# The recurrence's two projections as three products of rounded halves, in place of one 32-bit product

## The reference, cut to what matters

```
y      = layernorm(x1)                                # (8, 512, 256)
v      = y @ W_write.T                                # "values", 256 -> 256
read_t = alpha * sum over s < t of gamma^(t-1-s) * (y_t . y_(s-1)) * v_s       # in each head
s      = y + read @ W_read.T                          # "mix", 256 -> 256
```

## Time and profile before

| | us |
|---|---|
| median of 3 runs (3278.1 to 3281.41) | 3280.44 |
| the profiled execution | 3278.38 |
| its span, first to last instruction | 3276.6 |
| recurrence phase, from its first instruction to the first of the next phase | 1977.8 to 2152.8 |
| TensorE busy over the span | 3081.6 (94%) |

### The profile page before, as it was taken

One profiled execution on the slowest core, in us unless ns is written; L12 is line 12 of the kernel. 1 busy time (PEld: TensorE's weight loads), 2 busy tenths in 40 slices (PEclk: granted clock), 3 DMA queues, 4 the chain that ended last, 5 costly groups with the idle time before them and its releaser, 6 DMA issues. The chain is left out here.

```text
span 3276.6 us, 74792 instructions
## 1 busy us (share of the span) xinstructions
PE 3081.6 (94%) x22540; PEld 2326.4 (71%) x22540; DVE 2156.3 (66%) x6507; ACT 1932.9 (59%) x4816; POOL 1154.6 (35%) x1806
## 2 busy tenths in 40 slices
PE   8979999999999999989999997969999965999995
PEld 6756666666666666668888884536666655999995
DVE  4338888888888888876666655547777636333334
ACT  4437777777777777765565553226766653333333
POOL 2104444444444444443333330034242202333331
PEclk9989999999999999999999998979999967999998
DMA  8863332222333233243333342111111133223225
GB/s 265 279 198 83 82 80 82 81 78 79 89 84 81 80 82 81 77 161 117 128 128 135 109 140 66 39 51 31 37 47 36 44 119 103 37 38 89 37 40 172
DMA packets 200831, 309.98 MB, mean 95 GB/s; under 512 B 36242, under 2 KB 144530, under 8 KB 200434
## 3 DMA queue, kind: packets, MB, share of 16 engines
q1 hardware_dynamic: 187826, 290.54, 29.0%
q0 software_dynamic: 12864, 17.57, 3.2%
HBM read 208.03 MB, written 90.31 MB: 91 GB/s over the span
## 5 line engine op out<-in xcount | busy, mean ns | idle before, releaser
L993 POOL TENSOR_SCALAR at_p<-at_p,at_recip 128x512 f32<-128x512 f32 (+3 forms) x1030 | 538.4, 541 | 630.0 <-DVE at_recip L1105 630.0
L1031 ACT ACTIVATE at_p<-at_p,at_nmax 128x512 f32<-128x512 f32 (+3 forms) x1032 | 570.5, 555 | 253.2 <-DVE at_nmax L1099 253.2
L1099 DVE CUSTOM_DVE_ANT_0 at_p<-at_s_ps,at_bias 128x512 f32<-128x512 f32 (+3 forms) x1032 | 459.7, 488 | 56.3 <-PE at_s_ps L1211 39.7
L1211 PE MATMUL at_s_ps<-at_k_twice,at_q 64*128 64x512 f32 (+3 forms) x3096 | 343.6, 341 | 8.2 <-DVE at_nmax L1099 6.7
L2057 DVE CUSTOM_DVE_ANT_0 aa_a_ps<-aa_a_ps,aa_hidden 128x128 f32<-128x128 f32 (+3 forms) x512 | 242.4, 511 | 102.2 <-PE aa_a_ps L2219 100.0
L1233 PE MATMUL at_o_ps<-at_pT,at_v 128*64 128x512 f32 (+3 forms) x2064 | 307.2, 440 | 0.0
L1111 DVE COPY at_pT<-at_t_ps 128x512 f32<-128x512 f32 (+3 forms) x512 | 239.5, 488 | 88.6 <-PE at_t_ps L1223 86.0
L1957 ACT ACTIVATE aa_pT<-aa_b_ps 128x512 f32<-128x512 f32 (+1 forms) x384 | 196.2, 530 | 140.6 <-PE aa_b_ps L2237 138.0
L1223 PEld LDWEIGHTS at_t_ps<-ident,at_p 64*128 64x128 f32 x5120 | 189.0, 138 | 118.0 <-issue 118.0
L1233 PEld LDWEIGHTS at_o_ps<-at_pT,at_v 128*64 128x64 f32 x2064 | 136.9, 137 | 186.5 <-issue 167.9
L663 ACT ACTIVATE nw_h<-nw_h_ps,nw_b 128x512 f32<-128x512 f32 x192 | 132.2, 689 | 211.4 <-PE nw_h_ps L767 211.0
(11 more groups left out here) (325 smaller groups left out, 7443.5 us busy)
## 6 DMA issues: line engine op xcount, KB each, us to landing
at_k_twice<-k_dram SPq DMA_DIRECT2D x260, 256.0 KB, 3.8
k_dram<-ln_keys SPq DMA_DIRECT2D x128, 256.0 KB, 3.8
nw_w_raw<-in_w_all_dram SPq DMA_DIRECT2D x26, 1024.0 KB, 5.0
nw_w_raw<-in_w_all_dram SPq DMA_DIRECT2D x52, 512.0 KB, 6.7
at_v<-v_dram SPq DMA_DIRECT2D x129, 128.0 KB, 2.0
v_dram<-ln_values SPq DMA_DIRECT2D x16, 1024.0 KB, 5.7
w_all<-in_w_dram SPq DMA_DIRECT2D x12, 768.0 KB, 9.2
nw_xh<-xh_dram SPq DMA_DIRECT2D x10, 512.0 KB, 4.4
```

The source lines that it names most:

```text
L993: pool.tensor_scalar(p, p, recip[:, u:u + 1], 1.0, ALU.mult, ALU.mult).then_inc(scaled, 1)
L1031: act.activation(p_sb[:, u, 0:N], p_sb[:, u, 0:N], ACT.Exp, bias=nmax[:, u:u + 1], scale=-1.0, accum_out=total[:, u:u + 1]).then_inc(exped, 1)
L1099: dve.tensor_tensor_reduce(out=p_sb[:, u, 0:N], in0=s_ps[u % 2][:, score_at(u // 2)], in1=bias[:, u % 2, S - N:S], scale=1.0, scalar=BIG, ...
L1211: ins = pe.matmul(s_ps[h][:, score_at(j)], qst[par][rows, q, at], k_twice[par][rows, k, 0:N], start=(i == 0), stop=(i == 2))
```

## The change

The values are formed as y_high w_high + y_high w_low + y_low w_high, and the mix in the same way, 12 products a half where there were 4. ScalarE's copy of a read now writes the rounded high part; VectorE subtracts it from the sum in PSUM (`rest_read`) and mix waits for that. GpSimd splits both weights and, for every sample, the turned rows yT into `yh` and `yl`; `values` waits for it. On VectorE `rest_read(n-1,1)` is put behind decay_pair(n,0,0), `rest_read(n,0)` behind decay_pair(n,1,2). The semaphores of `network_phase` are cleared by GpSimd in the recurrence (23 names, some in pairs), since two more are needed.

```diff
@@ -475,7 +475,7 @@
     with ExitStack() as ctx:
-        sb, ps, sem = hold(ctx, nc)
+        sb, ps, sem = hold(ctx, nc, spent_too)
         w1_raw = [w1_early, sb("nw_w1_raw1", [P, KT, HID])]
@@ -1310,7 +1310,10 @@
         prod = sb("rc_prod", [P, RH, sum(WIDTHS)])
-        readT = sb("rc_readT", [P, KT, S])
+        readh, readl = (sb(f"rc_read{x}", [P, KT, S], F32R) for x in "hl")
+        yh, yl = ([sb(f"rc_y{x}{i}", [P, KT, S], F32R) for i in range(2)] for x in "hl")
+        wwh, wwl = (sb(f"rc_ww{x}", [P, KT, D], F32R) for x in "hl")
+        wrh, wrl = (sb(f"rc_wr{x}", [P, KT, D], F32R) for x in "hl")
         s_sb = [sb(f"rc_s{i}", [P, TT, D]) for i in range(2)]
@@ -1340,6 +1343,8 @@
         read_out = sem("rc_read_out")
+        read_low = sem("rc_read_low")
+        split = sem("rc_split")
         mixed = sem("rc_mixed")
@@ -1351,6 +1356,10 @@
             return (n * KT + g) * TT + t
+
+        def y_done(n):
+
+            return 4 * n + (8 if n else 6)
@@ -1385,10 +1394,35 @@
+            def split_w(hi, lo, raw, n):
+                pool.tensor_scalar(hi[:], raw[:], 1.0, 1.0, ALU.mult, ALU.mult).then_inc(split, 1)
+                pool.wait_ge(split, 6 * n + 1)
+                pool.tensor_tensor(lo[:], raw[:], hi[:].bitcast(F32), ALU.subtract).then_inc(split, 1)
+
+            def split_y(n):
+                for k in range(KT):
+                    pool.wait_ge(turn_out, KT * n + k + 1)
+                    if n >= 2:
+                        pool.wait_ge(valued, 2 * (n - 1))
+                    pool.tensor_scalar(yh[n % 2][:, k, :], yT[n % 2][:, k, 1:S + 1], 1.0, 1.0, ALU.mult, ALU.mult)\
+                        .then_inc(split, 1)
+                    pool.wait_ge(split, y_done(n) + (2 * k - 3))
+                    pool.tensor_tensor(yl[n % 2][:, k, :], yT[n % 2][:, k, 1:S + 1], yh[n % 2][:, k, :].bitcast(F32),
+                                       ALU.subtract).then_inc(split, 1)
+
+            pool.wait_ge(w_loaded, 32)
+            split_w(wwh, wwl, ww, 0)
+            split_y(0)
             for h in range(RH):
...
                                    base=-1, pattern=[[1, S]], channel_multiplier=-1).then_inc(pool_chain, 1)
+            for done_with in spent:
+                pool.sem_clear(done_with)
+
+            split_w(wrh, wrl, wr, 1)
+            for n in range(1, B):
+                split_y(n)
@@ -1420,7 +1454,9 @@
                 act.wait_ge(read, 2 * n + g + 1)
-                act.activation(readT[:, g, :], r_ps[g][:], ACT.Copy).then_inc(read_out, 1)
+                if n > 0:
+                    act.wait_ge(mixed, 2 * n)
+                act.activation(readh[:, g, :], r_ps[g][:], ACT.Copy).then_inc(read_out, 1)
@@ -1485,6 +1521,10 @@
+            def rest_read(n, g):
+                dve.wait_ge(read_out, 2 * n + g + 1)
+                dve.tensor_tensor(readl[:, g, :], r_ps[g][:], readh[:, g, :].bitcast(F32), ALU.subtract).then_inc(read_low, 1)
+
             def finish(n, half):
@@ -1510,6 +1550,7 @@
                 if n > 0:
+                    rest_read(n - 1, 1)
                     finish(n - 1, 0)
@@ -1524,9 +1565,11 @@
                 decay_pair(n, 1, 2)
+                rest_read(n, 0)
                 decay_pair(n, 1, 3)
...
                     norm(n + 2)
+            rest_read(B - 1, 1)
             finish(B - 1, 0)
@@ -1545,11 +1588,13 @@
                 pe.wait_ge(turn_out, KT * n + KT)
+                pe.wait_ge(split, y_done(n))
                 for i in range(2):
-                    for k in range(KT):
-                        at = 1 + (2 * half + i) * P
-                        ins = pe.matmul(n_ps[half][:, i * D:i * D + D], yT[n % 2][:, k, at:at + P], ww[:, k, :],
-                                        start=(k == 0), stop=(k == KT - 1))
+                    at = (2 * half + i) * P
+                    for a, (x, w) in enumerate([(yh, wwh), (yh, wwl), (yl, wwh)]):
+                        for k in range(KT):
+                            ins = pe.matmul(n_ps[half][:, i * D:i * D + D], x[n % 2][:, k, at:at + P], w[:, k, :],
+                                            start=(a == 0 and k == 0), stop=(a == 2 and k == KT - 1))
                 ins.then_inc(valued, 1)
@@ -1568,7 +1613,7 @@
                     if n > 0:
-                        pe.wait_ge(read_out, 2 * (n - 1) + g + 1)
+                        pe.wait_ge(read_low, 2 * (n - 1) + g + 1)
                 for h in range(2):
@@ -1578,21 +1623,23 @@
             def mix(n, half):
-                pe.wait_ge(read_out, 2 * n + 2)
+                pe.wait_ge(read_low, 2 * n + 2)
+                pe.wait_ge(split, 8)
                 if n + 1 < B:
...
                 for i in range(2):
-                    for g in range(KT):
-                        at = (2 * half + i) * P
-                        ins = pe.matmul(n_ps[half][:, i * D:i * D + D], readT[:, g, at:at + P], wr[:, g, :],
-                                        start=(g == 0), stop=(g == KT - 1))
+                    at = (2 * half + i) * P
+                    for a, (x, w) in enumerate([(readh, wrh), (readh, wrl), (readl, wrh)]):
+                        for g in range(KT):
+                            ins = pe.matmul(n_ps[half][:, i * D:i * D + D], x[:, g, at:at + P], w[:, g, :],
+                                            start=(a == 0 and g == 0), stop=(a == 2 and g == KT - 1))
                 ins.then_inc(mixed, 1)
...
                 turn(0, k)
-            pe.wait_ge(w_loaded, 32)
+            pe.wait_ge(split, 2)
             for half in range(2):
@@ -2992,13 +3039,13 @@
             network_phase(nc, x, w1_all, w2_all, b1_all, b2_all, ident, rows, coef, w1_early, w2_early, early_loaded,
-                          xh_dram, xl_dram, acc, x1_dram, spent)
+                          xh_dram, xl_dram, acc, x1_dram, spent, spent_too)
         with ExitStack() as layer1:
...
             r1 = sb("r1", [P, B * TT])
-            recurrence_phase(nc, x1_dram, w_write, w_read, decay, log_alpha, ident, y, r1, s_dram)
+            recurrence_phase(nc, x1_dram, w_write, w_read, decay, log_alpha, ident, y, r1, s_dram, spent_too)
             attention_phase(nc, w_proj, w_out, g1, ropes, spreads, ident, y, r1, recip_dram, moe_dram)
```

More of the change, by code:

```diff
@@ L467, in network_phase @@
 def network_phase(nc, x_dram, w1_all, w2_all, b1_all, b2_all, ident, rows, coef, w1_early, w2_early, early_loaded,
-                  xh_dram, xl_dram, acc, x1_dram, spent):
+                  xh_dram, xl_dram, acc, x1_dram, spent, spent_too):
     R = B * NF
     with ExitStack() as ctx:
-        sb, ps, sem = hold(ctx, nc)
+        sb, ps, sem = hold(ctx, nc, spent_too)
         w1_raw = [w1_early, sb("nw_w1_raw1", [P, KT, HID])]
@@ L1285, with recurrence_phase @@
 EPS_RMS = 1.1920928955078125e-07
-def recurrence_phase(nc, x1_dram, w_write, w_read, decay, log_alpha, ident, y, r1, s_dram):
+def recurrence_phase(nc, x1_dram, w_write, w_read, decay, log_alpha, ident, y, r1, s_dram, spent):
     with ExitStack() as ctx:
@@ L2973, in recurrent_kernel @@
         ident = sb("ident", [P, P])
-        spent = []
+        spent, spent_too = [], []
         with ExitStack() as layer0:
```

## The result

The changed kernel takes 3291.53 us in the median of 6 runs (3287.85 to 3293.95), the kernel before 3279.27 in 6 runs beside it (3274.82 to 3282.09). The ratio is 1.0036, with a 95% interval of 1.0024 to 1.0048: slower by 12 us. The profiled execution took 3291.64 us, its span 3289.8. The recurrence phase lasts from 1977.4 to 2163.5, 186.0 us where it was 175.0.

A forecast was written before the change was run, and what follows sets the result against it. TensorE, busy all through, bounds the recurrence. Start +2.0, sample 0 -0.64, samples 1 to 6 +4.9, sample 7 +1.5, end +0.1 make +7.8; one clock fall gives +9.4 us, forecast 3290, range 3279 to 3298.

The forecast's parts named there:

- The products: Each half of values and mix: twelve float32r products take 1.61 us where it was 1.93, saving 0.32, -1.28 a full sample.
- The new wait: Before the first mix of samples 1 to 7: TensorE stands 2.1 us for the remainder behind VectorE's decays.
- GpSimd's splits: Steady samples: GpSimd's 4.08 us of splitting fits in 5.3 us of cover and costs nothing; upper bound +4 us.
- rival 4: Values of the next sample wait for GpSimd's late split: +0.5 us a sample, +4 in all, 3294; chance 0.12.
- The start: Start of the phase: values(0) wait for GpSimd until 1992.3, then run at half clock; +2.0 us, bounds -0.5 and +2.3.
- The clock: TensorE behind the new stops: one fall to half clock as the likeliest, +1.6 us.
- Sample 7 and the end: Sample 7 saves only on one mix, +1.5 us; at the phase's end the remainder against the cheaper last mix, +0.1.
- Rival 2: Halves of values and mix: edges vanish, a group takes 1.28 us, saving cancels the wait; -2.8 us, 3277.6; chance 0.12.
- rival 3: VectorE's queue before mix: VectorE is through early and no stop forms; sum -6.9 us, 3273.5; chance 0.06.
- rival 1: TensorE's clock falls behind most stops before mix, 4 to 7 falls: +14 to +19 us, 3294 to 3299; chance 0.12.

## Why the prediction was right

The forecast was 3290, with a range of 3279 to 3298; it came to 3291.5. By its own steps:

- *The products.* A group of twelve took 2007.15 to 2008.77 at full clock, 1.62 us, 1.61 was forecast from the earlier trace rows. TensorE's work in a sample fell by 19.55 - 18.41 = 1.14 as the profile counts it busy, where 1.28 was forecast. The Trainium skill's figure (TensorE: Matmul & The Clock Gate, section Back-to-back issue gap), an estimate of 109 ns and a group of 1.52, is 0.10 under the measured group; the row was the better source.
- *The new wait.* 2.04 us later (3.10 against 1.06), 2.1 forecast, from the order on VectorE alone; moving one call took 1.6 of it away. A sample came to 20.38, forecast 19.55 + 0.82 = 20.37. That the two agree to 0.01 is luck: TensorE was idle for 1.97 and not 2.1, and its work fell by less than forecast, and the two errors cancel.
- *GpSimd's splits.* 3.56 us busy a sample and nobody waits for them: forecast right for the steady samples, rival 4 fell. By the Trainium skill (GPSIMD Engine Reference, section Key points) GpSimd contends with VectorE instructions that have two SBUF inputs or are in a two-port mode. The trace agrees as far as it goes: the decays, with one input in PSUM, took 684 ns in the mean and 683 before, and the remainder, which reads PSUM too, 682. What the prediction left out is the other side: norm, which reads no PSUM, was held up at the start, one instruction for 1.44 us beside GpSimd's difference of a weight. No run shows in which mode it was.
- *The start.* values(0) at 1991.96, forecast 1992.3; half clock through them; dots(0,0,0) at 1997.35, forecast 1998.1. From the phase's beginning to dots(1,0,0) it took 35.70 us and 34.30 before: +1.4, forecast 2.0 - 0.64 = +1.4. Against the second profile of before (32.8) it is +2.9, since the half clock that I let go there had not come at all in that run. So this agreement hangs on which execution of the kernel before was profiled.
- *The clock.* One fall forecast at 1.56, two came at 1.52 each: the size was right, the number one short. My evidence was one row; a second profile shows two again.
- *Sample 7 and the end.* From the last sample's first dots to the next phase 25.0 us against 23.4, forecast +1.6.

In sum +1.4, six samples +5.0, two falls +3.0, the end +1.6: 11.0, and the phase grew by 186.0 - 175.0 = 11.0, which is 1.6 over the forecast 9.4, the price of the second fall. Against 173.5, which two of the three profiles with the old products show, it grew by 12.5. The medians differ by 12.3, the two profiled executions by 13.3, of which 2.6 lie behind the phase. The prediction had no term for that part, and whether it belongs to the change is open.

Rival 2 (wait and saving cancel) fell with the 1.62 us of a group, rival 3 (the wait does not form) with the 1.97 us before each mix, rival 1 with two falls in place of four to seven.

## What to carry to other kernels

When a cheaper operation needs an extra step on another engine, look at what stands ahead of that step in the engine's queue, not at its own 0.7 us: here two decays, which themselves waited for TensorE, made it a stop of 2 us a sample, 14 us in all against 10 saved. The step belongs ahead of work that depends on the engine which will wait for it, and the engine that waits should be given other work first; both together turned 12 us of loss into 7 of gain. Idle time on an engine that was full all through is paid in full, and it can cost the clock besides. A new instruction on an engine with time to spare can still delay its neighbour: here GpSimd's difference of a weight made an instruction of VectorE last 1 us longer.

## What the runs showed of the hardware

- A stop of TensorE of 1.97 us was followed by 3.4 us at 0.50 in two of seven places, in both profiles of the changed kernel, and in one of seven with the mix alone; it cost 1.5 us each time. Filled down to 0.68 us of idle time, none was followed by it. In the other profiles stops of 1.73 and 2.65 us were followed by 3.4 us of it and one of 3.04 us by 6.8; stops of 1.34, 1.02, 0.80 and 0.36 us by none.
- GpSimd can make an instruction of VectorE last more than three times as long: of four tensor_scalar instructions of VectorE (128x256, SBUF only, 0.41 us each) one took 0.71 us beside GpSimd's rounding of 128x512 (0.72) and one 1.43 us when GpSimd's difference of 128x512 (1.26) began with it. So it was in the first kernel with sample 0's values in 32 bits, and nearly so in six others; with GpSimd made to wait all four took 0.41.
- Changing between the 64-row dots and full products costs TensorE about 0.2 us each time: with two changes fewer a sample went from 18.41 us of work to 18.04.
